# Filler products into free PSUM banks where TensorE waits: layer 0, layer 1's cross-attention, layer 3's cross-attention

## The reference, cut to what matters

```
# layer 0: ten tokens of each batch item are picked and replaced
scores = x @ score_w + score_b;  _, idx = top_k(scores, 10)
sparse = x[idx];  q = sparse @ Wq.T + bq;  k, v = ctx @ Wk.T + bk, ctx @ Wv.T + bv      # 16 heads of 8
x = x.at[idx].set(softmax(q k^T / sqrt(8)) v @ out_w.T + out_b)
# layer 1: one head of 128, post-norm
y = layer_norm(y + attention(y, y, WQ1, WK1, WV1, causal=True), g1, be1)
y = layer_norm(y + attention(y, ctx, WQ2, WK2, WV2, causal=False), g2, be2)
y = layer_norm(y + relu(y @ W_ff1 + b_ff1) @ W_ff2 + b_ff2, g3, be3)
# layer 2: 16 heads of 8, rotary, pre-norm: causal self, cross, gelu feed-forward
# layer 3: 16 heads of 8, q, k, v and the softmax fake-quantised to 8 bits: self, cross to ctx, gated feed-forward
sim = fq(q) fq(k)^T * 8**-0.5;  out = fq(softmax(sim)) fq(v)
```

## Time and profile before

| | us |
|---|---|
| median of 3 runs | 538.43 |
| lowest, highest | 537.33, 538.61 |
| the profiled execution, its own time | 533.29 |
| its span, first to last instruction | 531.4 |
| mean granted TensorE clock over the span | 0.811 |
| PE, DVE, ACT, POOL busy | 416.6, 355.2, 253.8, 241.9 |

### The profile page before, as it was taken

One profiled execution on the slowest core, in us unless ns is written; L12 is line 12 of the kernel. 1 busy time (PEld: TensorE's weight loads), 2 busy tenths in 40 slices (PEclk: granted clock), 3 DMA queues, 4 the chain that ended last, 5 costly groups with the idle time before them and its releaser, 6 DMA issues.

```text
span 531.4 us, 8266 instructions
## 1 busy us (share of the span) xinstructions
PE 416.6 (78%) x2836; PEld 209.5 (39%) x2840; DVE 355.2 (67%) x802; ACT 253.8 (48%) x513; POOL 241.9 (46%) x378
## 2 busy tenths in 40 slices
PE   6979768889888999998988872566664766779897
PEld 3735645644434433434243550222231222324546
DVE  1644665466999411329584469999989898679552
ACT  2213524225000566751626327899977784456441
POOL 4033124348100244451401315999989798236420
PEclk9758976999999999999999995555555555566999
DMA  9400000000000000000000002699786688113301
GB/s 260 163 1 1 4 0 1 1 0 1 1 2 1 0 1 3 0 2 0 1 0 2 2 1 39 134 145 151 147 140 92 127 136 160 29 25 75 74 1 39
DMA packets 88975, 26.10 MB, mean 49 GB/s; under 512 B 81061, under 2 KB 88167, under 8 KB 88935
## 3 DMA queue, kind: packets, MB, share of 16 engines
q1 hardware_dynamic: 88935, 25.58, 25.1%
HBM read 5.61 MB, written 0.52 MB: 12 GB/s over the span
## 4 chain that ended last, share of the span: by engine, by line
PE 43%; DVE 27%; POOL 19%; issue 5%; ACT 4%; DMA 1%; POOLq 0%; DVEq 0%; ACTq 0%
POOL k_stack L573 12%; DVE k_stack L2088 8%; PE ps L842 5%; PE ps L857 4%; POOL stats L564 3%; PE ps L643 3%; PE ps L744 3%; DVE stats L2168 3%; DVE xh L1659 2%; PE ps L754 2%; DVE st L1650 2%; POOL rstd L483 2%; PE ps L818 2%; PE ps L630 2%; PE ps L920 1%
## 5 line engine op out<-in xcount | busy, mean ns | idle before, releaser
L2168 DVE TENSOR_REDUCE stats<-ps 128x2 f32<-128x1024 f32 x64 | 77.7, 1214 | 2.4 <-PE ps L1313 2.0
L1615 ACT ACTIVATE e_buf<-ps,stats,sders 128x512 f32<-128x512 f32 x88 | 67.6, 773 | 18.5 <-POOL stats L564 18.5
L1333 PE MATMUL ps<-k_stack,q_stack 128*32 128x128 bf16 x512 | 38.1, 306 | 38.7 <-DVE k_stack L2181 38.7
L573 POOL TENSOR_SCALAR k_stack<-e_buf,stats 128x512 int16<-128x512 f32 x88 | 63.0, 728 | 2.1 <-DVE stats L2175 1.5
L1461 ACT ACTIVATE e_buf<-ps 128x1024 f32<-128x1024 f32 (+3 forms) x44 | 28.2, 711 | 58.3 <-PE ps L842 58.3
L1333 PEld LDWEIGHTS ps<-k_stack,q_stack 128*32 128x32 bf16 x512 | 21.8, 128 | 69.2 <-DVE k_stack L2181 66.4
L430 POOL TENSOR_SCALAR_AFFINE_SELECT e_buf<-e_buf 128x256 f32<-128x256 f32 x44 | 17.8, 412 | 65.9 <-ACT e_buf L1461 65.2
L481 POOL TENSOR_SCALAR rstd<-mv 128x4 f32<-128x4 f32 x18 | 4.4, 243 | 93.7 <-DVE mv L1653 93.7
L1313 PE MATMUL ps<-q_stack 32*128 32x512 bf16 x128 | 37.2, 581 | 12.4 <-ACT e_buf L1615 8.9
L2088 DVE TENSOR_REDUCE k_stack<-ps 128x4 f32<-128x1024 f32 (+3 forms) x32 | 44.8, 1484 | 2.5 <-PE ps L801 2.5
L842 PE MATMUL ps<-k_stack,q_stack 32*128 32x512 f32 (+3 forms) x256 | 34.7, 478 | 0.6 <-ACT e_buf L1461 0.4
(11 more groups left out here) (281 smaller groups left out, 898.0 us busy)
## 6 DMA issues: line engine op xcount, KB each, us to landing
wsq<-in_squares SPq DMA_DIRECT2D x3, 384.0 KB, 4.9
k_stack<-k_stack SPq DMA_TRANSPOSE x64, 3.1
spread<-in_spread SPq DMA_DIRECT2D x1, 896.0 KB, 6.7
x<-in_x SPq DMA_DIRECT2D x1, 512.0 KB, 4.3
l_w<-in_L_xattn_W_ff SPq DMA_DIRECT2D x2, 256.0 KB, 7.1
l_w<-in_L_xattn_fc_w SPq DMA_DIRECT2D x2, 256.0 KB, 7.7
l_w<-in_L_xattn_ff_w SPq DMA_DIRECT2D x1, 512.0 KB, 8.7
out<-x SPq DMA_DIRECT2D x2, 256.0 KB, 2.3
```

The source lines that it names most:

```text
L573: pool.tensor_scalar(t_rows[n % TURNING][:, j, :], e_ring[n % len(e_ring)][:, j, :], stats[:, 2, c:c + 1], 0.0, ALU.mult, ALU.add).then_in ...
L1333: mm = pe.matmul(ps[BAND * band:BAND * (band + 1), 7, qb * P:(qb + 1) * P], v_band[:, kb, b, V * band + v, :], t_keys[n % len(t_keys)][:, ...
L1615: act.activation(e_ring[n % len(e_ring)][:, j, :], ps[:, 2 * (n % 3) + j, :], ACT.Exp, bias=stats[:, 1, c:c + 1], scale=sders[:, 8:9], acc ...
L2168: dve.tensor_reduce(stats[:, 0, c:c + 2], ps[:, 2 * (n % 3):2 * (n % 3) + 2, :], AX, ALU.max, negate=True).then_inc(S("ints.nm"), 1)
```

## The change

The change adds calls of `keep_warm` and three waits on TensorE; nothing is removed and no other engine's program differs. Layer 0 gets 25 products in eight calls (2, 2, 2, 1, 10, 2, 4, 2 in order), 3 more stand behind layer 1's projections, `single_head` gets 6, 6, 6, 5 and 4, the last pairs of layer 3's self-attention 1 each for `n` = 60 to 63 and 2 for `n` = 64, and layer 3's cross-attention 11 at tile 2, 4 and 7 at tile 4, and 3 each at tiles 5, 6 and 7. That is 92 products in all. New waits: `heads.base` (GpSimd has zeroed `k_stack`) and `L0.kept` (VectorE has read bank 2) in layer 0, and `L3.ca.q` at the last pairs.

```
+WARM_FROM = PAIRS - 4
...
                 pe.wait_ge(S("L0.x"), QB)
+                zeros = k_stack[:, 8 * NT:8 * NT + N]
+                keep_warm(0, 6, zeros)
                 turn_half(xh, "L1.ln1.xh", 0)
...
                 scores(T)
+                keep_warm(0, 6, zeros)
                 for i in range(T + 1, T + QB):
                     steps(i)
+                keep_warm(0, 6, zeros)
                 turn_half(xh, "L1.ln1.xh", 1)
...
                 scores(T + QB + 1)
+                keep_warm(0, 5, zeros)
                 turn(T + QB)
...
+                keep_warm(0, 4, zeros)
                 turn_half(xh, "L1.ln2.xh", 0)
...
                             subtract(i - 1)
+                            keep_warm(6, 4, half(q_int, 0))
                             pe.wait_ge(S("cross.q"), B)
...
+                        if i == 2:
+                            keep_warm(6, 11, half(q_int, 0))
...
+                        if i == QB:
+                            keep_warm(6, 7, half(q_int, 0))
...
                             outputs(i - FLAT_VALUES_BEHIND)
+                        if QB < i < T:
+                            keep_warm(7, 3, half(q_int, 0))
                         if i < T:
                             turned_maxima(i)
...
+            pe.wait_ge(S("heads.base"), 1)
+            keep_warm(3, 2, zeros)
             pe.wait_ge(S("L0.rank"), 1)
...
             mm.then_inc(S("L0.rankT"), 1)
+            keep_warm(3, 2, zeros)
             pe.wait_ge(S("L0.onehot"), 1)
...
+            pe.wait_ge(S("L0.kept"), 1)
+            keep_warm(2, 2, zeros)
             pe.wait_ge(S("L0.picked.sb"), 1)
...
             turn_picked(0)
+            keep_warm(2, 1, zeros)
             pe.wait_ge(S("L0.qblk"), 1)
...
             turn_picked(1)
+            keep_warm(2, 10, zeros)
             pe.wait_ge(S("L0.p"), 1)
...
+            keep_warm(2, 2, zeros)
             pe.wait_ge(S("L0.pt"), 1)
...
+            keep_warm(2, 4, zeros)
             pe.wait_ge(S("L0.oT"), 1)
...
+            keep_warm(2, 2, zeros)
             pe.wait_ge(S("L0.ao"), 1)
...
+                keep_warm(0, 3, zeros)
                 pe.wait_ge(S("L1.sa.v"), B)
...
                     if n >= VALUES_BEHIND:
+                        if WARM_FROM <= n <= PAIRS:
+                            pe.wait_ge(S("L3.ca.q"), 1)
+                            keep_warm(6, 1 + n // PAIRS, half(k_int, 0))
                         int_outputs(n - VALUES_BEHIND)
```

18 lines of the change are left out of this document (added).

## The result

The changed kernel takes 521.14 us (median of 4 runs, 519.95 to 523.01) beside 537.92 (537.33 to 538.61) for the kernel before: ratio 0.9691, 95% interval 0.9652 to 0.9729. The forecast was 524.3, range 518.5 to 530.5. The profiled execution of the changed kernel took 520.02 us, its span is 518.2 and its mean granted clock 0.864, where the execution shown of before had 533.29, 531.4 and 0.811. The two traces are thus 13.2 to 13.3 us apart; the forecast for that pair was 14.1.

A forecast was written before the change was run, and what follows sets the result against it. TensorE at half clock was taken to bound layers 0 and 1 but hardly layer 3's self-attention. Gains 6.5 + 1.5 + 4.1 + 2.0 = 14.1 us off the 538.43 median gave 524.3, range 521 to 528, with rivals 518.5 to 530.5.

The forecast's parts named there:

- What bounds: Layers 0 and 1 are a chain through a half-clock TensorE; in layer 3's self-attention a faster TensorE gives little.
- Price of a filler: Each added product on TensorE takes 0.216 us at full clock, about 0.44 at half; zeros as operand hold the clock.
- Layer 0: 5.85 for 6.5: Layer 0, 18.8 to 46 us: products at full clock save 6.94, fillers cost 0.43; gain 6.5, ends 4 and 7.2.
- one fall remains: Clock still drops once, around layer 0's L1196, layer 1's tile 9 or layer 3's tile 3; gain 4.2 less, 528.5; chance 0.17.
- The cost put on the two fillers ahead of the ranks: Layer 0, ahead of L1191: the two fillers have no pause to hide in and delay the chain by 0.43 us.
- Layer 1: Full clock gains 1.5 us in layer 1's self-attention and 4.1 in its cross-attention, where all fillers fit the pauses.
- Layer 3: 1.90 for 2.0: Cross-attention: tile 4 gives 1.65, or 0.7 if the clock falls in tile 3; tiles 5 to 7 give 1.0; together 2.0.
- The total: Whole kernel: 14.1 us gained, profiled execution 533.29 to 519.2, median 538.43 to 524.3.
- more than forecast: Whole kernel: the median's extra 5.1 us may be further clock falls that fillers now hold; 519, chance 0.08.
- three signs that the prediction named: Half clock left before 300 us; fillers delaying a signalled product over 0.5 us; VectorE's or GpSimd's waits growing where TensorE's shrink.
- slower: Layers 0, 1 and 3: clock stays at half and fillers stand in front of the work; 17 us late, 555.5; chance 0.05.
- The rival by the Trainium skill's rule: Whole kernel: short pauses are not why the clock falls, so filling them changes nothing; 538.8, chance 0.05.

The follow-up runs named there:

- the second trace: The unaltered change measured once more against the kernel before, beside other kernels on one chip: 522.82 us, ratio 0.9777.

## Why the prediction was right

**What bounds.** The reading held: the clock lay on the chain in layers 0 and 1 (together 11.37 us less with fillers, 0.94 of them not the fillers' work) and hardly in layer 3's self-attention (1.3 us for a doubled clock over 61).

**Price of a filler.** 0.216 and 0.44 were near what was measured: 0.45 for two at full clock, and 0.427 from one to the next at half. An operand of zeros holds the clock as far as any filler here does: all fillers of layers 0 and 1 have it, and this trace has no fall in layer 1; the second trace has one, at tile 9. That more counts than being busy was argued from the thin products ahead of 20.93 and is shown by the two-row fillers. The description of those products was loose: L1191 has two weight rows and two columns, but L1187 has 512 columns and L1196 has 128 weight rows and ten columns.

**Layer 0: 5.85 for 6.5.** The stretch from the turned ranks to layer 1's first scores gave 5.53 of the 6.94; the start gave +0.32 where -0.43 was put, and the 0.94 us of the earlier first rise are in it. Without that accident layer 0 gave 4.91 for 6.5, so that 5.85 looks closer than the reasoning was. The stage splits as follows, with the trace that has no fall (tile 3 filled) beside it:

| from the start of one to the next | before | after | no fall | forecast gain |
|---|---|---|---|---|
| gather to queries | 3.08 | 2.24 | 2.23 | 1.0 |
| queries to turned probabilities | 5.68 | 5.68 | 4.90 | 0.65 and part of 1.0 |
| turned probabilities to output weight | 4.17 | 3.21 | 3.27 | rest of 1.0 |
| output weight to rows put back | 1.48 | 1.07 | 1.07 | 0.45 |
| rows put back to second projections | 8.00 | 4.68 | 4.68 | 3.84 |

The fall at 22.12 to 25.53 took 0.78, all that the queries' stage would have given: the rival "one fall remains" happened, at the place that it named, and cost a fifth of the 4.2 put on it, since the clock was back within 3.41 us. In the second trace two falls cost 1.29 and 1.24 us. The other miss is the largest term: 3.32 for 3.84. I counted 3.75 + 3.53 down to 3.44, but the two products take 1.91 and 1.95 at full clock, their tails included.

The cost put on the two fillers ahead of the ranks, 0.43 us, was mis-sized too. From the flags' start to the ranks' it takes 1.06 us where before takes 0.44, but that isn't the fillers: VectorE's step that the ranks wait for (L2008) ended at 18.84 and the ranks started at 18.91. The kernel with layer 1's fillers alone has none there and takes 1.05 us, waiting for VectorE:

```profile
18.56 0.41 PE L1197 MATMUL ps<-ident,e_buf 2*128 2x2 f32 x4 [0.45 <-DVE e_buf L1985]
```

In the change's second trace they did stand in the way: VectorE's step ended at 19.36 and the ranks started at 20.00. So the cost is 0 to 0.6 us, and it depends on how early the flags are beside VectorE.

**Layer 1.** 1.42 for 1.5 and 4.10 for 4.1, and the products behind the runs of fillers still wait 0.24 to 0.42 us for VectorE, so the fillers fitted; doubled they did not. The 1.42 of the self-attention also came in a kernel without a filler ahead of it (layer 1's fillers alone), so the number was right and the fillers' part in it is open.

**Layer 3: 1.90 for 2.0, in part by luck.** Tile 4 gave 0.70, the prediction's value with the clock fallen in tile 3. But its value without that fall, 1.65, is the step that failed: with tile 3 filled it is 0.79, and over tiles 2 to 4 no different from the change, because VectorE's work on the queries, which TensorE waits for, ends with GpSimd's scaling. I had treated the queries and tile 4's products as if TensorE alone stood on that chain. The 0.70 has another source: before, VectorE's row sums waited 0.60 us for ScalarE's exponentials of tile 2, behind products at half clock; at full clock they don't, GpSimd's scaling starts 1.65 us after tile 3's maxima for 2.35, and what hangs on it comes that much earlier. So the size was right and the cause was not.

Tiles 5 to 7 gave 1.19 for 1.0: tiles 5, 6 and 7 came 4.08, 4.31 and 4.31 us after the one before, forecast 4.35, with VectorE busy in

```profile
463.68:476.38 12.70, 9.92 (x69) 4.71 (x70) 12.29 (x28) 9.21 (x15) 8.58 (x5) 1.00 0.38 73
```

12.29 of 12.70 us, the bound that was named.

**The total.** For the pair of traces 13.2 for 14.1. The medians are 3.2 us under the forecast because the kernel before read 537.92 and its gain was 16.8, more than the traces show. That is the rival "more than forecast" in part, and the trace with layer 3's fillers alone shows how it can come about: with layers 0 and 1 as before, an execution can be 4.88 us later at the feed-forward's output rows than the one that the forecast was worked out from. How often that happens differs from one comparison to the next: before ranges from 531.1 to 538.8, the change from 519.9 to 524.6, and in the second comparison the medians are only 11.5 apart. That the time lies inside the stated range is owed to the range as much as to the sum.

**What would have shown it wrong.** Two of the three signs that the prediction named showed. PEclk was to read 1.00 to the end of layer 2; it fell once, at 22.12, and twice in the second execution. And fillers stood between a signal and the product that waited for it by more than 0.5 us in the second execution, 0.64 at the ranks and 0.82 at the turned probabilities. Both are the short falls and the unsteady start at work, and they cost 0.8 to 2.5 us of a gain that stayed. As for the sizes, L644's passes take 0.43 to 0.49 us each, the output-row product came 2.52 earlier for 2.8, the feed-forward's first product 10.04 for some 11. (The "slower" rival's 3.87 us of idle in the cross-attention is 17.06 - 13.14 = 3.92; nothing hangs on it.)

**The rival by the Trainium skill's rule** (TensorE: Matmul & The Clock Gate, "Why this matters for your kernels"). Given 0.05: filling pauses of 0.4 to 1.9 us would bring nothing. The pair of traces is 13.2 us apart, and both comparisons have the change faster, so on this point the traces decide against it.

## What to carry to other kernels

Read the granted clock before any engine's busy share, and then ask stage by stage whether TensorE is on the chain: holding the clock gave some 10.4 us in layers 0 and 1 (11.37 less the 0.94 of an earlier start) and 1.3 over 61 us of layer 3. If it is, full-height products into a free bank, sized to just under the wait that they stand in front of, hold the clock but for short falls; count them, since twice as many cost 7 us. Where TensorE waits for another engine, look at what that engine waits for as well: at tile 4 a faster TensorE only made VectorE's step wait longer. Where the clock falls differs between executions of one kernel, so compare stages in traces and medians over many runs, and don't read one trace's fall as a property of the place.

## What was not expected of the hardware

- A busy TensorE can stay at half clock: 23.90 of 23.90 us with two-row fillers between thin products. What the runs show is that the rows of a product matter; how much of anything is enough they don't show.
- One program's clock falls in other places from one execution to the next, each short fall of 3.4 us at a cost of nothing (tile 3), 0.8 and 1.3 (queries and scores of layer 0, in the change's two traces: 5.68 and 6.19 us from queries to turned probabilities, 4.90 without a fall), 1.24 (tile 9) or 1.7 us (dense products). The kernel before ranges over 1.4%, with mean clocks of 0.793 to 0.816.
- The first rise came at 11.15 to 14.18 us in the fourteen traces, and the flags of layer 0 started at 17.50 to 18.93 us, the later the rise the later the flags, but for differences of up to 0.13 us. That is up to 1.4 us which no filler here touches.
- A VectorE step of 0.48 us took up to 1.78 us beside GpSimd's scaling of 2.25 us, and in all fourteen traces ended 0.27 to 0.29 us after it. What ties the two together the traces don't show.
